# Gate term and residual formed early, the first batch's ending moved into attention, and more row maxima in the gated stage

## What is computed

```python
x = L0_attn_x                                   # [2, 1024, 512]
xn = _layernorm(x, axis=-1)
s = attn(xn)     # 32 heads of 16, causal, ALiBi, softmax; then  @ w_out.T + b_out
g = _silu(ffn(xn))   # ternary octonion weights: silu(gate) * up (1366 -> 1360 rows), then down
x = x + s * g
```

```python
scores = jnp.einsum('bqhd,bkhd->bhqk', q, k) * scale + alibi
scores = jnp.where(causal, scores, -1e9)
attn = jax.nn.softmax(scores, axis=-1)
out = jnp.einsum('bhqk,bkhd->bqhd', attn, v)
```

## Time and profile before

| | us |
|---|---|
| three runs | 896.7, 898.8, 901.62 |
| median | 898.8 |
| the profiled execution's own time | 896.58 |
| span of its trace, first to last instruction | 894.8 |
| mean granted TensorE clock | 0.979 |

### The profile page before, as it was taken

How to read it: one execution, slowest core, us unless ns; L and a number is a source line. 1 busy time by engine, 2 the same in 40 slices (tenths; PEclk the granted TensorE clock), 3 DMA queues, 4 the chain that set the end, 5 groups by cost and what they waited for, 6 DMA issues and landing times.

```text
span 894.8 us, 16075 instructions
## 1 busy us (share of the span) xinstructions
PE 816.8 (91%) x5938; PEld 355.9 (40%) x5938; DVE 630.1 (70%) x1795; ACT 479.1 (54%) x631; POOL 112.7 (13%) x124
## 2 busy tenths in 40 slices
PE   5899989999999999999899899999999999998866
PEld 4445444444444334334343333333333333333322
DVE  5475786643242463463799999999999999992498
ACT  4453265333232221231587778887877778789310
POOL 3123131323031121121000000000000000000042
PEclk8899999999999999999799999999999999999989
DMA  7735322243102000000022111222222111264658
GB/s 218 210 107 177 129 72 82 100 123 94 48 1 71 24 1 24 24 0 30 19 63 75 56 55 55 70 75 75 66 71 75 50 58 56 72 193 125 226 192 314
DMA packets 68199, 80.01 MB, mean 89 GB/s; under 512 B 26630, under 2 KB 38918, under 8 KB 67608
## 3 DMA queue, kind: packets, MB, share of 16 engines
q1 hardware_dynamic: 67992, 78.71, 27.8%
q0 software_dynamic: 128, 0.27, 0.2%
HBM read 46.95 MB, written 31.73 MB: 88 GB/s over the span
## 4 chain that ended last, share of the span: by engine, by line
PE 64%; DVE 16%; issue 8%; DMA 7%; SPq 4%; ACT 2%; POOL 0%; ACTq 0%; DVEq 0%
PE psum L1389 13%; PE psum L1349 9%; PE psum L1412 9%; PE psum L1413 8%; DVE mshown L1083 5%; PE psum L1423 4%; PE psum L1424 4%; DVE mx L1087 4%; PE psum L1365 3%; DMA o_scr<-osum 2%; PE psum L1249 2%; PE psum L1251 2%; PE psum L1250 2%; DMA r_scr<-den 2%; PE psum L1261 2%
## 5 line engine op out<-in xcount | busy, mean ns | idle before, releaser
L806 ACT ACTIVATE probs<-psum,exp_scale 128x1024 f32<-128x1024 f32 (+1 forms) x320 | 311.8, 1028 | 78.4 <-PE psum L1374 48.5
L1083 DVE CUSTOM_DVE_ANT_0 mshown<-psum,ahead 128x384 bf16<-128x384 f32 (+3 forms) x512 | 221.9, 487 | 15.2 <-PE psum L1349 13.9
L1349 PE MATMUL psum<-QKs 51*128 51x512 f16 (+3 forms) x768 | 194.1, 333 | 16.0 <-DVE mx L1083 6.2
L1389 PE MATMUL psum<-probs,Vs 128*32 128x512 f32 (+3 forms) x1536 | 162.3, 510 | 19.8 <-ACT osum L812 17.6
L1087 DVE TENSOR_REDUCE mx<-psum 128x1 f32<-128x512 f32 x256 | 158.6, 683 | 3.2 <-PE psum L1349 2.2
L1365 PE MATMUL psum<-QKs 53*128 53x512 f16 (+3 forms) x768 | 139.5, 331 | 3.3 <-ACT probs L806 3.1
L1412 PE MATMUL psum<-X,room 128*128 128x512 f16 (+1 forms) x352 | 133.9, 380 | 0.0
L1413 PE MATMUL psum<-X,room 128*128 128x512 f16 (+1 forms) x352 | 133.4, 379 | 0.0
L1349 PEld LDWEIGHTS psum<-QKs 51*128 51x128 f16 x768 | 53.2, 94 | 166.4 <-DVE mx L1083 87.8
L831 ACT ACTIVATE room<-psum,gate_half 128x512 f32<-128x512 f32 (+1 forms) x44 | 30.2, 687 | 110.0 <-PE psum L1413 109.9
L1117 DVE SCALAR_TENSOR_TENSOR room<-room,psum 128x512 f32<-128x512 f32 (+1 forms) x44 | 30.2, 687 | 71.3 <-ACT room L831 71.3
(11 more groups left out here) (148 smaller groups left out, 934.4 us busy)
## 6 DMA issues: line engine op xcount, KB each, us to landing
o_scr<-osum SPq DMA_DIRECT2D x32, 256.0 KB, 2.9
QKs<-q_scr SPq DMA_DIRECT2D x96, 64.0 KB
QKs<-k_scr SPq DMA_DIRECT2D x96, 64.0 KB
q_scr<-qk_stage SPq DMA_DIRECT2D x16, 256.0 KB, 2.2
k_scr<-qk_stage SPq DMA_DIRECT2D x16, 256.0 KB, 2.2
v_scr<-v_stage SPq DMA_DIRECT2D x16, 256.0 KB, 2.0
Vs<-v_scr SPq DMA_DIRECT2D x16, 256.0 KB
g_scr<-room SPq DMA_DIRECT2D x16, 256.0 KB, 2.0
```

What stands on the lines that cost most here:

```text
L806: nc.scalar.activation(probs[n % PSLOTS][:, 2 * pair:2 * pair + 2, 0:COLS[n]], s_bank[pair][:, :, 0:COLS[n]], ACT.Exp, scale=exp_scale[:, ...
L1083: last = nc.vector.tensor_tensor_reduce(out=mshown[at % 2][:, cols], in0=m_bank[bank][:, cols], in1=ahead[:, CH - keys:], scale=1.0, scala ...
L1349: last = nc.tensor.matmul(tile[:, hh, :], Qs[s][rows, pair + hh, qb * P:(qb + 1) * P], Ks[s][rows, pair + hh, k0:k0 + keys], start=(hh == ...
L1389: last = nc.tensor.matmul(pv_bank[32 * h:32 * h + 32, CH - cols:CH], Vs[s][:, kb, h::QH], probs[n % PSLOTS][:, h, at:at + cols], start=(kb ...
```

## The change

1. **Early gate term.** After each down tile DVE does two more operations (in `gated`): y = g times the down scale times b_out, and y plus x. x is loaded once into the probs buffers before attention, y is kept in DRAM (y_scr, one more store per down tile on SP). `finish` then is gate = (PSUM x fin_scale) x gate, and base + gate, both on DVE; the bias operation and the POOL additions at the end go.
2. **A fourth set** of queries, keys and values (SLOTS = 4); its queries and keys lie in X160, which the gated stage reads until its third chunk. `load(3)` is issued in the gated stage's last chunk.
3. **More maxima early.** 122 instead of 52 items lie in the gated stage (123 with one that is left out), three after each second ffn tile from the 24th on. A quad has 37 instead of 42 maxima, in a new GROUP string. `load(t + 3)` is issued at the first scores of quad t.
4. **The first batch's ending inside attention.** Chunks 0 and 1: sums and denominators are loaded in quad 9, inverted at quad 10, reciprocals loaded in quads 11 and 12, and POOL multiplies and splits them (24 operations). In the last quad twelve pieces of six projection matmuls (`project`, six token tiles) stand between the score pieces. ACT's `high_attention` is gone; DVE does the split of chunks 2 and 3.
5. **The last batch's ending** is cut by rows: three quarters of chunks 2 and 3 (kt 0 to 2) are fetched during quads 14 and 15, the last quarter after the last quad. The projection of the last four tiles is split the same way.

```diff
-SLOTS = 3
+SLOTS = 4
-GROUP = "MPMMPSMMSMPMMSSMMMSSMMPMSMMSPMMSMPMM" \
-        "SMSMMPMSMMMMSSMPMMSPMMSSMMPMMSMSMMSM"
+GROUP = "MPMSMMPMSMSMPMMSSMMPMSMMSPMMSMPMM" \
+        "SSMMPMSMMSMPSMMSMPMSMMSMPMSMSMMSMS"
+AHEAD = [LEAD + (QUADS - 2 - t) * (NITEM - GROUP.count("M")) for t in range(QUADS - 1)]
 def work_order():
-    early = [(0, i) for i in range(NITEM) if i != ROWS_AT] + [(1, i) for i in range(LEAD)]
+    early = [divmod(i, NITEM) for i in range(line(0)) if i != ROWS_AT]
...
-        due = max(n + 1 - F_FIRST, 0) * len(early) // (len(tiles) - F_FIRST)
-        order += [("maximum", *x) for x in early[given:due]]
-        given = max(given, due)
+        if tile[1] % 2 and len(tiles) - n <= 2 * -(-len(early) // MRING):
+            order += [("maximum", *x) for x in early[given:given + MRING]]
+            given += MRING
...
+            if t == QUADS - 1 and w[0] == "scores":
+                behind += 1
+                if 2 <= behind < 2 + PIECES:
+                    n, part = divmod(behind - 2, 2)
+                    order.append(("project", n, part * KT // 2, (part + 1) * KT // 2))
...
+    order += [("project", n, 0, KT) for n in range(PIECES // 2, 3 * TT)]
+    order += [("project", n, 0, KT_EARLY) for n in range(3 * TT, 4 * TT)]
+    return order + [("project", n, KT_EARLY, KT) for n in range(3 * TT, 4 * TT)]
...
-                    if n == 0 and SLOTS - 2 <= t <= QUADS - 3:
-                        load(t + 2)
+                    if n == 0 and 1 <= t <= QUADS - SLOTS:
+                        load(t + SLOTS - 1)
...
             def gated(j, p):
+                nc.vector.scalar_tensor_tensor(out=y_stage[d % 2], in0=g_stage[d % 2], scalar=down_half[:, 0:1], in1=bo_row[:],
+                                               op0=ALU.mult, op1=ALU.mult).then_inc(y_step, 1)
+                nc.vector.tensor_tensor(y_stage[d % 2], y_stage[d % 2], x_rows[j][:, t - HT, :], ALU.add).then_inc(y_done, 1)
...
+            def finish(n):
+                nc.vector.scalar_tensor_tensor(out=gate[c][:, t, :], in0=banks[PROJ_BANKS[n]], scalar=fin_scale[:, 0:1], in1=gate[c][:, t, :],
+                                               op0=ALU.mult, op1=ALU.mult).then_inc(gated_done, 1)
+                nc.vector.tensor_tensor(base[c][:, t, :], base[c][:, t, :], gate[c][:, t, :], ALU.add).then_inc(fin_done, 1)
...
+            def project(n, k0, k1):
+                for kt in range(k0, k1):
+                    nc.tensor.matmul(bank, high[:, kt, tok], OW[:, 0, kt, :], start=(kt == 0), stop=False)
+                    nc.tensor.matmul(bank, high[:, kt, tok], OW[:, 1, kt, :], start=False, stop=False)
+                    last = nc.tensor.matmul(bank, low[:, kt, tok], OW[:, 0, kt, :], start=False, stop=(kt == KT - 1))
```

More of the change, by code:

```diff
@@ L569, in reciprocals @@
[L569 to L592, removed]
@@ L607, in _ @@
[L607 to L615, removed]
+                    if w[2] == 1 and w[1] == NCH - 1:
+                        sp.wait_ge(f_filled, (NCH - 2) * FTILES + 2 * HT)
+                        constants(SLOTS - 1)
+                        load(SLOTS - 1)
+            for w in ORDER[:ORDER.index(("scores", QUADS - 1, 0, 0))]:
+                beside(w)
@@ L626, in _ @@
[L626 to L639, removed]
+            denominators(3, KT_EARLY, KT)
@@ new lines, in _, with out_row @@
+            sums(3, KT_EARLY, KT, num_late[3])
+            sp.wait_ge(den_done, 6)
+            inverted(3, KT_EARLY, KT)
+            sp.wait_ge(rec_stored, 6 * 16)
+            reciprocals(3, KT_EARLY, KT, rec_late[3])
+            def out_row(n):
+                c, t = divmod(n, TT)
+                sp.wait_ge(fin_done, n + 1)
+                sp.dma_start(outf[n * P:(n + 1) * P, :], base[c][:, t, :]).then_inc(fin_stored, 16)
+            for n in range(NCH * TT):
+                out_row(n)
@@ new lines, in _ @@
+            invert(2, 0, KT_EARLY, 4)
+            invert(3, 0, KT_EARLY, 4)
+            dve.wait_ge(fin_ready, 1)
+            finish(0)
+            finish(1)
+            attended(2, 0, KT_EARLY, (num_loaded[2], rec_loaded[2]))
+            finish(2)
+            for kt in range(KT_EARLY):
+                parted(2, kt, kt)
+            finish(3)
+            attended(3, 0, KT_EARLY, (num_loaded[3], rec_loaded[3]))
+            finish(4)
+            for kt in range(KT_EARLY):
+                parted(3, kt, 3 + kt)
@@ L1186, in _ @@
+            invert(2, KT_EARLY, KT, 5)
+            finish(5)
+            attended(2, KT_EARLY, KT, (num_late[2], rec_late[2]))
+            parted(2, KT_EARLY, 6)
+            finish(6)
+            finish(7)
+            invert(3, KT_EARLY, KT, 6)
+            finish(8)
+            finish(9)
+            finish(10)
+            attended(3, KT_EARLY, KT, (num_late[3], rec_late[3]))
+            parted(3, KT_EARLY, 7)
+            for n in range(11, NCH * TT):
+                finish(n)
         @block.tensor
```

321 lines of the change are left out of this document (196 added, 125 removed).

## The result

The changed kernel takes 920.5 us (median of four, 918.8 to 925.7) against 898.7: a ratio of 1.025, 95% interval 1.021 to 1.029. The forecast was 868, with 850 to 888 as its range; the time lies 32.5 us above the range, on the side that had 5%.

What follows compares the result with a forecast made beforehand. DVE with its 42 maxima was taken to bound the quads, PE close behind. From 896.6: gated stage +4, quads -36, load waits +11, clock +6, last quad and ending -14.5, median +1, giving 868 us, range 850 to 888.

Steps and rivals of the forecast that it cites:

- The quads: Quads 0 to 14: five fewer maxima each bring a quad from 25.3 to 22.9 us, -36 us in all (-21 to -46).
- The 0.9: DVE's wait per quad, in us, behind PE's wait for ACT's output copy; claimed to stay as it was.
- both its ends: Bounds of a quad's forecast time: 22.2 us from DVE plus its wait, 23.9 from PE's busy time and waits.
- the slow rival: Quads already bound by PE, so fewer maxima free nothing: quads stay at 25.3 us, 904 us in all; chance 0.05.
- The load waits and the clock behind them: Quads 1 to 3: PE stalls for the new set, +11 us (0 to 20), and slow clock after, +6 (0 to 10).
- The last quad and the ending: From the last quad's first scores to the end: 70 us instead of 84.4, -14.5 us (-17 to -6).
- The last quarter's chain: In the ending: copy, stores, loads, invert, multiply and split take some 17 us, covered by 23.3 us of projection.
- The gated stage: Stage before attention: 70 more maxima, in triples between tiles, lengthen it by 4 us (3 to 8).
- A step that I had at nothing: Gated stage: the 32 new operations of y lie beside down tiles of 4.75 us and are hidden, no cost.
- The first batch's ending beside quads 9 to 13: 24 POOL operations and some 6 MB of DMA lie beside these quads; DVE keeps its pace, no cost.
- The wide reading of the rule on the shared port: Quads 9 to 13: POOL's SBUF contention read as slowing every DVE operation, 11 us; the forecast did not adopt it.
- the rows of the last quad: Before quad 15: PE's 3 to 4 us from maxima transpose to first scores about match the path, no cost.

## Why the prediction was wrong, point by point

**The quads, the step that failed.** The sum said "with the 0.9 us behind the output copy, which stays, 22.2 is the lower end", and 22.9 a quad for the rest. The 0.9 did not stay. I took a wait that one order of work had made for a property of the kernel, while the change rewrote the order. The new string puts two exponentials between product 2 and the copy. PE's wait became 1.6 to 2.4 us and DVE's behind it 2.4 in quad 5, in place of 0.9, and it costs its whole length. Three quads ran at full clock all the same, 5, 8 and 11, with waits of 2.4, 1.8 and 1.6 us: 25.7, 25.0 and 25.2 us, against 23.4, 23.1 and 23.5 with only that copy moved, so 2.3, 1.9 and 1.7 us more. That is 2.0 us a quad, 30 in 15 quads by this estimate. The other 12 of the 42.3 come in quads with a lower clock, such as quad 9 (second row, under quad 8; 24.9 with the copy moved):

```profile
672.04:697.03 24.99, 22.02 (x236) 8.89 (x235) 21.23 (x70) 20.43 (x23) 0.00 (x0) 1.00 0.23 65
...
697.03:725.03 28.00, 23.95 (x235) 8.88 (x233) 22.91 (x72) 20.56 (x23) 0.00 (x0) 0.94 0.48 150
```

It is not the smaller number of maxima that makes the wait dear: with 42 of them a longer wait costs its whole length as well (the copy later in the kernel before). What the new string did was to lengthen it.

With both copies moved, quads 4 to 8 take 22.6 us on average. The forecast of 22.9 and both its ends were sound for these quads of that kernel. No rival had this case: the slow rival reached 904 by way of PE as the bound, and PE was no bound (22.2 of 25.7 us busy). Its number came nearer than its mechanism.

**The load waits and the clock behind them.** Taken as 11 + 6 = 17 us, measured as 15.3 with the copies early. Predicted were idle times of 7 and 3.5 us in quads 1 and 2 before a maximum of the new set; the trace has 5.7 and 2.9.

**The last quad and the ending.** Taken as 70 us (35 and 35), measured 36.4 + 33.5 = 69.9. The last quarter's chain was in time: PE waits 0.9 us in all of the ending, before a split (`room`, L1223):

```profile
898.47 0.39 PE L1539 MATMUL psum<-OW,room 128*128 128x512 f16 x1 [0.91 <-DVE room L1223]
```

**The gated stage.** Taken as +4 us, with 3 to 8 as its bounds: 254.3 against 247.8, +6.5, within them. A step that I had at nothing was wrong: at the stage's end the two operations of y stand before the maxima on DVE, and PE waits 3.1 us where it waited 1.58:

```profile
440.93 0.60 PE L1441 MATMUL psum<-QKs 51*128 51x512 f16 x1 [3.08 <-DVE mx L1153]
```

The stage also began 3.1 us later (182.7 instead of 179.6), which no term had. The other traces began it at 180.1 to 184.4, and the kernel before with the late copy, which is untouched up to there, at 183.0, so it need not be the change's.

**The first batch's ending beside quads 9 to 13.** Taken as nothing. With both copies early these five take 24.9, 23.5, 23.1, 23.5 and 23.7 us, 5.7 us more in all than five of 22.6. Under the old string only quad 9 is longer, by 1.45. For quad 9 the trace shows a cause, which no run took away: the term counted POOL's work and the DMA, and left out the two `invert` operations (L1209) that DVE does between maxima. PE waits behind them, and a product 4 us later takes 1.53 instead of 1.10 us (timeline of DVE, then PE, of that variant):

```profile
686.63 1.76 DVE L1209 RECIPROCAL den<-den 128x128 f32<-128x128 f32 x2
```

```profile
689.08 0.33 PE L1441 MATMUL psum<-X 51*128 51x384 f16 x1 [1.59 <-DVE mx L1153]
```

```profile
693.00 1.53 PE L1481 MATMUL psum<-probs,Vs 128*32 128x512 f32 x8
```

The masked maxima kept their pace beside POOL: 0.422 us for 256 columns between 734 and 746 us, when POOL works all the time, and 0.420 between 560 and 680, when it is idle (groups by form):

```profile
L1153 DVE CUSTOM_DVE_ANT_0 mshown<-psum,ahead 128x256 bf16<-128x256 f32 x4 | 1.5, 422 | 0.8 <-PE psum L1441 0.8
```

```profile
L1153 DVE CUSTOM_DVE_ANT_0 mshown<-psum,ahead 128x256 bf16<-128x256 f32 x36 | 13.1, 420 | 0.6 <-PE psum L1441 0.6
```

The wide reading of the rule on the shared port, with its 11 us, is out. The Trainium skill, GPSIMD Engine Reference, section Specifications, names contention only with DVE instructions in a two-port mode or with two SBUF inputs; the trace agrees, as far as these maxima go. What lengthens quads 10 to 13 by 0.5 to 1.1 us each is not shown.

**Quad 14 and the rows of the last quad.** The rows were taken as nothing, and quad 14 as one of 15 that get 2.4 us shorter. But by `line` and AHEAD it has 31 maxima and the transposition in both kernels: nothing was taken out of it. From quad 13's last copy to the first scores of the last quad the kernel before needs 19.2 us, the changed one 24.2, and the variant with both copies early 21.7. PE waits for the parts of the maxima before their transposition, with half clock behind it:

```profile
847.15 0.31 PE L1434 MATMUL psum<-ident,mparts 128*96 128x128 f16 x1 [1.98 <-DVE mparts L1171]
```

**The account,** for the traced execution. The sum put its span at 865.3 us; it was 923.7, so 58.4 are to be explained. Ahead of attention 7.2: 3.1 of late start, 2.5 in the gated stage, 1.6 more at its end. In attention 51.2 (412.8 instead of 361.6): the variant with both copies early needs 365.6 for it (441.1 to 806.7 us), so 47.2 go with the copies (42.3 by the medians) and 4.0 are left. These 4.0 hold the 5.7 beside quads 9 to 13 and the 5 of quad 14 (21.7 where 19.2 - 2.4 was forecast), less quads that ran under 22.9 us and the load waits. The last quad and the ending give nothing.

## What to carry to other kernels

When a change rewrites the order of work, no wait of the old trace may be carried over as a constant: for each buffer with one copy, write out what stands between its last writer, its evacuation and its next writer, on every engine, before and after. Tie an evacuation to the event that makes the buffer readable, not to a place in another stream that a new order moves. And follow a wait that an edit should remove: it can come back under another name with the same length, as in the kernel before with the copies earlier, and then the run says nothing of its price.

## What the runs showed of the hardware

Waits of PE of about 2 us, one in each quad, were in most cases followed by stretches at half clock: mean granted clock 0.92 between 570 and 806 us of the kernel before with the copy one exponential later, where waits of 1.1 us in the same places left it at 1.00:

```profile
570.00:806.00 236.00, 213.22 (x2068) 81.92 (x2062) 204.43 (x714) 171.96 (x187) 0.00 (x0) 0.92 0.21 60
```

```profile
570.00:806.00 236.00, 215.87 (x2229) 87.94 (x2229) 224.02 (x787) 190.05 (x205) 0.00 (x0) 1.00 0.26 76
```

I had read half clock behind a wait of 1.6 us in the old trace, and still priced it only for the load waits. It isn't regular: of the 16 waits of 2.0 to 2.2 us for the late copy in the kernel before, 14 had less than full clock right behind them and two had not, those of quads 2 and 11; the wait of 2.41 us in quad 5 of the changed kernel was followed by full speed, and the one of 1.98 before the transposition by half.
